# Cross-attention with image tokens on one core: a prologue laid out anew

## The reference

```
q    = x @ w_q
k, v = text @ w_k,  text @ w_v
ki,vi= image @ w_k_ip, image @ w_v_ip
out  = softmax(q k^T / 4) v  +  softmax(q ki^T / 4 + mask(bbox)) vi
y    = out @ w_out + b_out + x
```

## Time and profile before

| what | value |
|---|---|
| time, median of 3 runs | 246.53 us (244.32 to 246.85) |
| the profiled execution | 243.46 us |
| its span, first to last instruction | 241.5 us |
| mean granted TensorE clock | 0.921 of full |
| busy: PE, DVE, ACT, POOL | 191.8, 166.2, 127.3, 90.8 us |
| start of the transposes of the first maxima | 55.33 us |

### The profile page before, as it was taken

How to read it: one execution, slowest core, us unless ns; L and a number is a source line. 1 busy time by engine, 2 the same in 40 slices (tenths; PEclk the granted TensorE clock), 3 DMA queues, 4 the chain that set the end, 5 groups by cost and what they waited for, 6 DMA issues and landing times.

```text
span 241.5 us, 4536 instructions
## 1 busy us (share of the span) xinstructions
PE 191.8 (79%) x1608; PEld 156.7 (65%) x1608; DVE 166.2 (69%) x375; ACT 127.3 (53%) x289; POOL 90.8 (38%) x99
## 2 busy tenths in 40 slices
PE   0799999794897509986989699959869974998962
PEld 0699999793864408665767578747657754775741
DVE  0679893557267145985797598859867875879593
ACT  4554852223394234934784387359347732767750
POOL 6021220004420780548063726544482332645320
PEclk9999999996799955999799979999997995899999
DMA  6998369975877594169429843963594295011111
GB/s 210 381 323 297 120 181 181 262 249 111 277 182 199 165 171 142 65 153 216 125 71 190 185 138 98 203 174 133 129 180 125 78 196 103 4 57 64 54 57 54
DMA packets 34213, 38.04 MB, mean 157 GB/s; under 512 B 10096, under 2 KB 31344, under 8 KB 34032
## 3 DMA queue, kind: packets, MB, share of 16 engines
q1 hardware_dynamic: 34192, 37.76, 60.0%
HBM read 25.96 MB, written 11.80 MB: 156 GB/s over the span
## 4 chain that ended last, share of the span: by engine, by line
DMA 34%; PE 32%; DVE 14%; SPq 10%; issue 4%; ACT 3%; POOL 1%; DVEq 0%; POOLq 0%
PE bank L419 12%; DMA key_w<-shift_dram 9%; DMA q_dram<-q_l 8%; DMA qs<-shift_dram 8%; DVE negmax L1002 7%; PE bank L511 6%; PE bank L488 5%; SPq L287 4%; SPq L303 3%; PE bank L524 3%; PE bank L552 3%; PE bank L566 3%; DMA vip_dram<-vipn 2%; DMA shift_dram<-shift 2%; DMA ks<-k_dram 2%
## 5 line engine op out<-in xcount | busy, mean ns | idle before, releaser
L1002 DVE TENSOR_REDUCE negmax<-bank 128x4 f32<-128x448 f32 x80 | 49.8, 622 | 30.9 <-PE bank L488 30.5
L792 ACT ACTIVATE raw<-bank 112x512 f32<-112x512 f32 x80 | 45.9, 601 | 24.1 <-PE bank L511 23.8
L1153 POOL TENSOR_TENSOR x_l<-x_raw,x_h 128x512 fp32r<-128x512 f32 x8 | 11.1, 1390 | 61.8 <-ACT x_h L735 61.8
L511 PE MATMUL bank<-key_w 100*112 100x256 f32 x80 | 18.3, 326 | 13.8 <-DMA key_w<-shift_dram 13.8
L511 PE MATMUL bank<-qs,ks 100*112 100x256 f32 x80 | 17.5, 307 | 9.9 <-DMA qs<-shift_dram 9.4
L511 PEld LDWEIGHTS bank<-key_w 100*112 100x112 f32 x80 | 13.3, 208 | 15.6 <-DMA key_w<-shift_dram 14.8
L552 PE MATMUL bank<-raw,v 112*32 112x256 f32 x320 | 22.4, 387 | 1.3 <-DVE late L1045 0.8
L419 PE MATMUL bank<-ctx_hl,key_w 128*128 128x448 f32 x72 | 17.2, 403 | 7.4 <-DVE ctx_hl L930 7.4
L566 PE MATMUL bank<-raw,con 112*32 112x256 f32 x320 | 22.1, 382 | 0.0
L1204 POOL TENSOR_TENSOR late<-late 128x256 f32<-128x256 f32 x20 | 14.6, 729 | 19.8 <-DVE late L1045 19.8
L419 PE MATMUL bank<-wo_h,ctx_hl 128*128 128x320 f32 x80 | 19.7, 317 | 2.8 <-DVE ctx_hl L930 1.8
(11 more groups left out here) (102 smaller groups left out, 475.5 us busy)
## 6 DMA issues: line engine op xcount, KB each, us to landing
qs<-q_dram SPq DMA_DIRECT2D x12, 320.0 KB, 5.1
key_w<-q_dram SPq DMA_DIRECT2D x12, 320.0 KB, 5.1
x_raw<-xT SPq DMA_DIRECT2D x8, 384.0 KB, 7.2
q_dram<-q_h SPq DMA_DIRECT2D x8, 384.0 KB, 3.8
q_dram<-q_l SPq DMA_DIRECT2D x8, 384.0 KB, 2.7
late<-x SPq DMA_DIRECT2D x8, 320.0 KB, 3.2
out<-late SPq DMA_DIRECT2D x8, 320.0 KB, 6.4
ks<-k_dram SPq DMA_DIRECT2D x24, 75.0 KB, 3.3
```

Of the source, the lines that this page charges most:

```text
L511: mm = pe.matmul(banks[p % len(banks)][0:TEXT, S * ab:S * ab + S], ks[k][0:STACK + SHIFT, p, ab, 0:TEXT], qs[k][0:STACK + SHIFT, p, :], st ...
L792: nc.scalar.activation(probs[:, p, :], b_banks(b)[p % len(b_banks(b))][0:TEXT, :], ACT.Exp, scale=SCALE).then_inc(p_done, 1)
L1002: nc.vector.tensor_reduce(negmax[:, t, :, 2 * g:2 * g + 2].rearrange("p a q -> p q a"), s[:, :, 0:TEXT].rearrange("p (q a) n -> p q a n", ...
L1153: sub = lambda o, a, b: nc.gpsimd.tensor_tensor(o, a, b, ALU.subtract)
```

## The change

Loads. The context is loaded in two parts: the columns of batches 0 to 3 chunk by chunk beside the key weights, those of batches 4 to 7 in one DMA behind the constants, x of batch 0 and `wq`. `wq`, `wv` and the image values of batch 0 get buffers of their own (`wq_raw`, `wv_raw`, `vr_first`), and `wv_ip` and `w_out` go into the old key weight buffers. The area for software DMA descriptors is cut to 1024 bytes.

TensorE: first half of the keys, image keys, Q of batch 0, second half of the keys, image values, Q of batch 1, then the first pass of batch 0 with V of batches 0 to 4 between its pieces, V of 5 to 7, then the transposes.

The low parts of `wv_ip`, `wv` and `w_out` are made by POOL (`late_splits`), counted in `late_high` and `late_low`. SP stores the keys of batches 0 and 1 when all three blocks of the first half and the image keys have their low parts, loads them, and only then stores Q of batch 0; the keys of 2 and 3 and of 4 to 7 follow in two groups, the latter ahead of the first shifts. x of batch 2 is loaded after the queries of batch 1. ScalarE casts x of batch 2 before the V copies, all eight of which stand at the end.

```
         for j in range(CC):
             splits.append((wk_ctx_in[j], 32, wk_h[:, j, :], wk_l[:, j, :], w_raw[:, 0, j, :]))
-            splits.append((wk_ctx_in[j], 32, ctx_h[:, j, :], ctx_l[:, j, :], ctx_raw[:, j, :]))
+            splits.append((wk_ctx_in[j], 32, *(t[:, j, half_keys[0]] for t in (ctx_h, ctx_l, ctx_raw))))
         splits.append((kip_in, 32, cip_h[:], cip_l[:], cip_raw[:]))
         splits.append((kip_in, 32, wkip_h[:], wkip_l[:], w_raw[:, 1]))
+        KIP_SPLIT = len(splits)
+        splits.append((wq_in, 16, wq_h[:], wq_l[:], wq_raw[:]))
+        Q_SPLIT = len(splits)
+        splits.append((ctx_in, 16, *(t[:, :, half_keys[1]] for t in (ctx_h, ctx_l, ctx_raw))))
         K_SPLIT = len(splits)
...
+        late_splits = [(vip_w_in, wvip_h[:], wvip_l[:], wvip_raw), (wv_in, wv_h[:], wv_l[:], wv_raw[:]),
+                       (wo_in, wo_h[:], wo_l[:], wo_raw)]
...
# SP
             sp.dma_start(con[:], consts).then_inc(con_in, 16)
             sp.dma_start(x_raw[:], xT[0]).then_inc(x_in, 16)
+            sp.dma_start(wq_raw[:], wq).then_inc(wq_in, 16)
+            sp.dma_start(ctx_raw[:, :, half_keys[1]], ctxT[:, :, half_keys[1]]).then_inc(ctx_in, 16)
             sp.dma_start(box[:].rearrange("p b m c -> p (b m c)"), bbox.partition_broadcast(P)).then_inc(box_in, 16)
+            sp.dma_start(wv_raw[:], wv).then_inc(wv_in, 16)
+
+            sp.wait_ge(high, KIP_SPLIT)
+            sp.wait_ge(low, KIP_SPLIT)
+            sp.dma_start(wvip_raw, wv_ip).then_inc(vip_w_in, 16)
+            sp.dma_start(wo_raw, w_out).then_inc(wo_in, 16)
...
             for m in range(XC):
-                sp.wait_ge(kh_done, 2 * m + 3)
-                sp.wait_ge(kl_done, 2 * m + 3)
+                sp.wait_ge(kh_done, XC + 1)
+                sp.wait_ge(kl_done, XC + 1)
                 store_keys(m, slice(0, 2))
-            store_queries(0, 0)
             sp.wait_ge(zeroed, 4)
             sp.wait_ge(k_stored, 16 * 2 * XC)
             for blk in range(3):
                 keys(0, 0, blk)
+            store_queries(0, 0)
             queries(0, 0)
-            store_keys(0, slice(2, B))
+            for m in range(XC):
+                store_keys(m, slice(2, B // 2))
+            store_queries(1, 1)
+            sp.wait_ge(vipn_done, 1)
+            sp.dma_start(vip_dram.rearrange("k b n -> (k b) n"), vipn[:]).then_inc(vipn_stored, 16)
             sp.wait_ge(zeroed, 5)
             sp.wait_ge(ks_in, 16 * 6)
             for blk in range(3):
                 keys(1, 1, blk)
-            store_queries(1, 1)
+            sp.wait_ge(qs_in, 16 * 3)
+            queries(1, 1)
             load_x(2)
...
-            load_vr(slice(0, 1), vr_first_in)
+            load_vr(vr_first[:].unsqueeze(1), slice(0, 1), vr_first_in)
+            for m in range(XC):
+                sp.wait_ge(kh_done, m + 5)
+                sp.wait_ge(kl_done, m + 5)
+                store_keys(m, slice(B // 2, B))
             store_shifts(0)
-            store_keys(1, slice(2, B))
             shifts(0, 0)
             load_x(3)
-            store_keys(2, slice(2, B))
-            load_vr(slice(1, B), vr_in)
+            sp.wait_ge(va_ready, B)
+            load_vr(vr[:, 1:B], slice(1, B), vr_in)
...
# TensorE
+            project_k(0)
+            image_keys()
             pe.wait_ge(high, Q_SPLIT)
             pe.wait_ge(low, Q_SPLIT)
-            pe.wait_ge(kl_done, 1)
+            pe.wait_ge(kl_done, 4)
             project_q(0)
-            pe.wait_ge(high, V_SPLIT)
-            pe.wait_ge(low, V_SPLIT)
-            pe.wait_ge(kl_done, 7)
-            for b in range(3):
-                project_v(b)
+            pe.wait_ge(high, K_SPLIT)
+            pe.wait_ge(low, K_SPLIT)
+            project_k(1)
             pe.wait_ge(ql_done, 2)
             image_values()
-            project_v(3)
             pe.wait_ge(vipn_done, 1)
             project_q(1)
+            pe.wait_ge(late_high, 2)
+            pe.wait_ge(late_low, 2)
+            pe.wait_ge(kl_done, 7)
             for n in range(2 * GROUPS):
                 score_a(0, 0, n)
-                if n % 2 and n < 8:
-                    project_v(4 + n // 2)
+                if n % 2:
+                    project_v(n // 2)
+            for b in range(5, B):
+                project_v(b)
...
# ScalarE, after the splits of the loads
+            for m in range(XC):
+                high_keys(m, 0)
+            high_image_keys()
             high_q(0, 0)
             high_q(0, 1)
             act.wait_ge(q_ready, 2)
             split_x(1)
-            act.wait_ge(high, len(splits))
-            act.wait_ge(low, len(splits))
-            for b in range(3):
-                copy_v(b)
+            act.wait_ge(k_ready, XC + 1)
+            late_split(0)
+            late_split(1)
+            for m in range(XC):
+                high_keys(m, 1)
+            late_split(2)
             act.wait_ge(vipn_ready, 1)
             copy(vipn[:], spare[1][0:B * IP, 0:DP]).then_inc(vipn_done, 1)
-            copy_v(3)
             high_q(1, 0)
             high_q(1, 1)
-            for b in range(4, B):
-                copy_v(b)
             act.wait_ge(q_ready, 4)
             split_x(2)
+            for b in range(B):
+                copy_v(b)
...
# VectorE
-            for n in range(K_SPLIT):
+            for n in range(KIP_SPLIT):
                 split(n)
             dve.wait_ge(con_in, 16)
             split_x(0)
+            split(Q_SPLIT - 1)
+            split(K_SPLIT - 1)
+            for m in range(XC):
+                low_keys(m, 0)
             dve.wait_ge(box_in, 16)
...
+            low_image_keys()
             low_q(0, 0)
             low_q(0, 1)
-            split(VIP_SPLIT)
             split_x(1)
+            for m in range(XC):
+                low_keys(m, 1)
             ones(0)
...
# POOL
             split_x(0)
+            split_x(1)
+            late_split(0)
+            late_split(1)
             pool.wait_ge(k_ready, 7)
             nc.gpsimd.memset(ks[1][:].bitcast(F32), 0.0).then_inc(zeroed, 1)
-            split_x(1)
+            late_split(2)
             split_x(2)
```

More of the change, by code:

```diff
@@ L139, in build @@
         kc_h, kc_l = kc[0:XC], kc[XC:]
+        half_keys = [slice(half * B // 2 * TEXT, (half + 1) * B // 2 * TEXT) for half in range(2)]
         box = sb("box", [P, B, BOX, 4])
@@ L185, in build @@
             sem(n) for n in ("x_in", "xres_in", "ks_in", "vr_first_in", "vr_in"))
-        high, low = sem("high"), sem("low")
+        high, low, late_high, late_low = (sem(n) for n in ("high", "low", "late_high", "late_low"))
+        ctx_in = sem("ctx_in")
         zeroed, ones_set, mask_ready, mask_step = (sem(n) for n in ("zeroed", "ones_set", "mask_ready", "mask_step"))
@@ L384, in _, with load_vr @@
                 keys(1, 1, blk)
[L385 removed]
+            sp.wait_ge(qs_in, 16 * 3)
+            queries(1, 1)
             load_x(2)
[L387 to L391, removed]
             sp.wait_ge(vipn_stored, 16)
[L394 removed]
+            def load_vr(target, batches, loaded):
                 for n in range(2):
[L397 removed]
+                    sp.dma_start(target[64 * n:64 * n + 64],
                                  vip_dram[:, batches].unsqueeze(0).to_broadcast([HPC, IP, batches.stop - batches.start, DP])
                                  ).then_inc(loaded, 16)
[L401 removed]
+            load_vr(vr_first[:].unsqueeze(1), slice(0, 1), vr_first_in)
[3 more added lines that the diff above has]
+                store_keys(m, slice(B // 2, B))
             store_shifts(0)
[L403 removed]
             shifts(0, 0)
             load_x(3)
[L406 to L408 removed]
+            sp.wait_ge(va_ready, B)
+            load_vr(vr[:, 1:B], slice(1, B), vr_in)
+            sp.wait_ge(k_stored, 16 * 6 * XC)
             every_step(sp, step)
@@ L422, in image_keys @@
             def image_keys():
-                pe.wait_ge(high, K_SPLIT)
-                pe.wait_ge(low, K_SPLIT)
+                pe.wait_ge(high, KIP_SPLIT)
+                pe.wait_ge(low, KIP_SPLIT)
                 for m in range(XC):
@@ L429, in image_keys, with project_k @@
                 mm.then_inc(k_ready, 1)
[L432 to L440, removed]
+            def project_k(half):
+                for j in range(CC):
+                    if half == 0:
+                        pe.wait_ge(high, 2 * j + 2)
+                        pe.wait_ge(low, 2 * j + 2)
+                    for m in range(XC):
+                        w_hi, w_lo = (w[:, j, m * P:(m + 1) * P] for w in (wk_h, wk_l))
+                        n = half_keys[half]
                         mm = three(bank[2 * m + half][:, 0:448],
@@ L447, in image_values @@
             def image_values():
-                pe.wait_ge(high, VIP_SPLIT)
-                pe.wait_ge(low, VIP_SPLIT)
+                pe.wait_ge(late_high, 1)
+                pe.wait_ge(late_low, 1)
                 three(spare[1][:, 0:DP],
```

(31 more changed lines are left out.)

41 lines of the change are left out of this document (18 added, 23 removed).

## The result

The changed kernel takes 256.44 us (median of 4 runs, 255.58 to 258.75) beside 245.43 us for the kernel before (4 runs, 243.41 to 246.85): ratio 1.047, 95% interval 1.036 to 1.058. It is slower, by 11.0 us where +6.6 was forecast. The profiled execution took 255.58 us, 12.1 more than the profiled one of before, with a span of 253.7. The time lies inside the stated range; the middle of the forecast is 4.4 us low.

A forecast was written before the change was run, and what follows sets the result against it. TensorE's own order bounds the prologue, then a loop through DRAM (transposes, shifts, next score) sets each step. 15.2 - 2.9 - 5.1 - 0.6 = +6.6 us: 250.1 profiled, 253.1 median; range 245.0 to 258.5.

The forecast's parts named there:

- rival C: Whole kernel much slower: x at 62, transposes at 72.5, half of the recovery fails; 257.7 us, chance 0.18.
- second flight: Second transposes of the maxima to step 1's first score: a settled 10.9 us instead of 16.0, so -5.1.
- First keys and the gate: Prologue: image keys ready at 15.3, done 19.2; first key store waits for their low parts, 26.8; 0.4 us won.
- Half clock for Q: TensorE after standing still from 19.2 to 26.8: Q takes 5.1 us instead of 2.83, done 31.9.
- First queries: Key stores, key loads, Q's stores, then query loads: first score at 47.0, 2.5 us later than before.
- image values, their copy, Q of batch 1 and its copies: 46.2: TensorE's prologue work after the second key half: 2.11, 0.5, 2.83 and 1.2 us, ending at 46.2.
- V behind x: Fifth V waits for batch 2's x, landing 59.6, copy done 60.9; transposes at 70.5, 15.2 us later.
- What comes back: Recovery after the first transposes: -2.9 and -5.1 us in two flights, and -0.6 of clock.
- First flight: First transposes of the maxima to the next step's first score: 7.4 us instead of 10.3, so -2.9.
- Later stages: After the second flight: TensorE's hole there shrinks from 8.9 to about 4, a little clock back, -0.6 us.
- A: Prologue, no gate: x lands before 56.6, V follow at full clock, transposes at 63.7; 246.3 us, chance 0.22.
- B: Whole kernel faster: every flight at its free price, no wait for x, transposes at 61.6; 242.6 us, chance 0.12.

The follow-up runs named there:

- e2: Changed kernel with VectorE's low parts of the image keys moved ahead of the mask: 254.73 us, ratio 1.045 to the kernel before.
- e1: Changed kernel with ScalarE's eight V copies put back ahead of the cast of batch 2's x: 251.44 us, ratio 1.031 to the kernel before.
- b3: Kernel before with batch 2's x loaded after batch 1's queries and cast before the last four V copies: 243.76 to 250.38 us beside 244.25.
- e4: Changed kernel with the image values load divided, batches 2 to 7 after batch 1's shifts: four runs, 254.18 to 259.29 us.
- b1: Kernel before with the image values load divided, batches 2 to 7 after batch 1's shifts: 240.97 us, ratio 0.991.
- b4: Kernel before with image values read back by one DMA over 128 partitions instead of two over 64: ratio 0.975 to the kernel before.

## Why the prediction was right, and where its sizes were off

The direction and the prologue's mechanism came out. The recovery did not, and the range held because it was wide enough to take in most of rival C. One of the prediction's own signs of being wrong appeared: the first score of step 1 came 32.4 us after the first transposes (73.07 to 105.43), where more than 30 was to tell against it. It points at the second flight, below.

**First keys and the gate.** Forecast 15.3, 19.2, 26.8 for image keys' start, their end and the image low parts; measured 15.99, 19.90, 26.6. The gain of 0.4 us for the key stores came out as 0.6 (26.71). e2 shows that the mask is what stands there. Half clock for Q: 5.11 against 5.1.

**First queries** at 46.28 (47.0): right. Q's store landed in 3.6 (4).

**POOL.** The late weights took 3.56 and 2.98 us (3.8 and, by the same rate, 3.2), image values began at 39.39 (39.3). I looked for what VectorE does to POOL and not for what POOL does to VectorE. The step "image values, their copy, Q of batch 1 and its copies: 46.2" is the first mis-sized one (its terms add up to 45.9): the low part was ready at 49.1, since the fills, which no term held, stood in the way, one pair for 5.82 us and the other for 1.47. I had moved POOL's work without asking which VectorE instructions would meet it.

**V behind x.** x forecast at 59.6, cast at 61.99; V at 63.20 (60.9); transposes 73.07 (70.5). The mechanism holds by e1 and b3, and 9.87 for four V is 7.0 plus 2.8 at a granted 0.69 (2.5 forecast). Of the lateness, 3.1 us are the later issue of x behind the fills; x's own flight took 6.4 and gave back some of it (7.2 forecast).

**What comes back.** First flight -2.1 (-2.9): the forecast took it from the shifts' transfers, and TensorE's Q of batch 2 at a low clock held it. The step that failed in size is "the second flight costs a settled 10.9": it measured 15.1. I had blamed the 1080 KB of key stores beside the image values load. With these gone the flight fell by 0.9 only. e4 and b1 show that the load alone holds it (10.3 and 10.6 without its rest), and b4 that its form is a part of this (12.9). The rows were there to be read: the load is issued at 64, and POOL waits for it until 79; that is 1344 KB in 15 us, with other transfers beside it, at a DMA share of 0.80 to 0.84 in the middle. Such a share is not that of a full queue.

**Later stages** gave 2.5 back, not 0.6. Both traces have the same work there and the clock differs from step to step; no run separates this.

**Rivals.** A fails by the 5.70 us wait, and B with it. C, at +11.2, is nearer to the measured +11.0 than the forecast, and not by its number only: it had x at 62 (61.9), transposes at 72.5 (73.07), Q's low part still 12.91 us in flight (12.0) and 6 us coming back (5.6 in the table). Its reason in the prologue was the wrong way round, though: POOL did not take 6.4 us beside VectorE, it made VectorE wait. Of the 5.5 us by which the profiled difference exceeds the forecast, 2.5 are the prologue, 0.8 the first flight, 4.2 the second, less the 1.9 that the later stages gave beyond it and the 0.1 of step 0.

## What to carry to other kernels

An order is only as early as the last item of its gate. The new prologue had the first keys computed 12.4 us before the old one had all of its own (15.8 against 28.2) and could store them 0.6 us sooner, since a mask stood in front of the counter. When a group of copies is moved behind a cast, look up which DMA that cast waits for, and where that DMA stands in its issuer's queue. Before a flight is called congested by bytes, compare its DMA share with 1: a load that lands late at 0.8 may be badly formed, as this one was, and here its form could be changed without moving any work.

## What the runs showed of the hardware

A gain in time can be lost to the clock. In e2 nearly the same work took 13.2 us at a granted 0.61 and, in the changed kernel, 9.0 at 1.00. The whole times of one kernel follow the mean granted clock roughly: on one chip the kernel before ran 240.59 us at 0.940, 242.68 at 0.927 and 243.97 at 0.909, but also 244.02 at 0.928. Single edits of 3 us at a milestone can therefore vanish at the end: milestones tell where an edit acts, and only whole times over several executions what it is worth.

VectorE's cast on 4 partitions took 5.82 us for two while POOL ran without a gap, and 1.47 to 1.48 otherwise. POOL's subtraction of 128x960 took 2.77 us there and 2.27 without the casts.

One load of 1344 KB over 128 partitions landed in 11.1 us at DMA shares of 0.96 to 1.00; two loads of 672 KB over 64 partitions each, with the same bytes, took 14.6 from their issue to the end of POOL's wait, at 0.80 to 0.84.
